# A four-layer conditional transformer: gelu once a job in place, its input added by VectorE, a plain float32 second product

## Time and profile before

| | us |
|---|---|
| median of 3 runs | 1162.45 |
| lowest, highest | 1158.63, 1163.27 |
| profiled execution: span | 1160.9 |
| TensorE busy (matmul records) | 1094.3 |
| TensorE weight loads | 703.3 |
| ScalarE busy | 800.4 |
| VectorE busy | 706.6 |
| GpSimd busy | 491.9 |

### The profile page before, as it was taken

The page is one execution under the profiler, slowest core; times in us unless marked ns, Lnnn a source line. Parts: engine busy times, 40 slices in busy tenths (PEclk is TensorE's granted clock), DMA queues, the critical chain, the costliest instruction groups (busy, mean ns, idle before and its releaser), DMA issues.

```text
span 1160.9 us, 19685 instructions
## 1 busy us (share of the span) xinstructions
PE 1094.3 (94%) x6717; PEld 703.3 (61%) x6717; DVE 706.6 (61%) x1484; ACT 800.4 (69%) x1336; POOL 491.9 (42%) x447
## 2 busy tenths in 40 slices
PE   8899999889898999999999999999999999999985
PEld 5576877655555565656657656566656566555442
DVE  6554447535256266234775865865865866898874
ACT  3563655477788778787687686687687686686763
POOL 3542742613543623644335553335344345254222
PEclk9999999899999999999999999999999999999997
DMA  7000001213222203321122231023031121232301
GB/s 234 20 26 28 2 10 31 62 38 94 60 64 73 75 1 82 84 58 35 28 75 73 69 83 42 15 65 82 23 88 29 39 55 51 56 84 55 83 12 36
DMA packets 36385, 64.45 MB, mean 56 GB/s; under 512 B 7208, under 2 KB 22312, under 8 KB 36288
## 3 DMA queue, kind: packets, MB, share of 16 engines
q1 hardware_dynamic: 36288, 63.20, 20.6%
HBM read 22.90 MB, written 2.12 MB: 22 GB/s over the span
## 4 chain that ended last, share of the span: by engine, by line
PE 73%; DVE 10%; ACT 8%; issue 6%; POOL 4%; POOLq 0%; ACTq 0%; DVEq 0%
PE rings L597 13%; PE AVB L709 13%; PE rings L598 11%; PE rings L599 11%; PE rings L696 10%; PE rings L671 5%; DVE m L1203 2%; PE rings L729 2%; ACT probs L891 2%; PE rings L734 2%; PE rings L640 1%; ACT L891 1%; DVE m L1183 1%; ACT gT_h L957 1%; PE rings L746 1%
## 5 line engine op out<-in xcount | busy, mean ns | idle before, releaser
L1203 DVE TENSOR_REDUCE m<-rings 128x1 fp32r<-128x512 f32 x512 | 319.0, 681 | 100.6 <-PE rings L671 73.3
L891 ACT ACTIVATE probs<-rings 128x512 f32<-128x512 f32 x562 | 292.9, 616 | 99.4 <-PE rings L671 71.1
L696 PE MATMUL rings<-SQ,SK 64*128 64x512 f32 x768 | 237.9, 446 | 14.7 <-ACT probs L888 6.3
L671 PE MATMUL rings<-SK,SQ 63*128 63x512 f32 x512 | 200.3, 457 | 5.4 <-ACT probs L891 4.2
L696 PEld LDWEIGHTS rings<-SQ,SK 64*128 64x128 f32 x768 | 109.0, 188 | 142.4 <-issue 55.1
L709 PE MATMUL AVB<-probs,V 128*32 128x512 f32 x1536 | 193.6, 611 | 0.0
L1306 POOL TENSOR_TENSOR gT_l<-gT_f,gT_h 128x512 fp32r<-128x512 f32 x96 | 121.4, 1286 | 75.7 <-ACT gT_h L957 73.8
L888 ACT ACTIVATE probs<-rings 128x1024 f32<-128x1024 f32 x103 | 101.0, 1037 | 34.2 <-PE rings L696 20.6
L597 PE MATMUL rings<-w_h,gT_h 128*128 128x256 f32 x384 | 110.2, 287 | 1.2 <-ACT gT_h L957 0.7
L671 PEld LDWEIGHTS rings<-SK,SQ 63*128 63x128 f32 x512 | 84.2, 184 | 39.7 <-ACT probs L891 33.1
L598 PE MATMUL rings<-w_l,gT_h 128*128 128x256 f32 x384 | 106.7, 278 | 0.0
(11 more groups left out here) (185 smaller groups left out, 2229.4 us busy)
## 6 DMA issues: line engine op xcount, KB each, us to landing
SQ<-qh SPq DMA_DIRECT2D x96, 128.0 KB, 2.6
SK<-kh SPq DMA_DIRECT2D x96, 128.0 KB, 2.8
SQ<-ql SPq DMA_DIRECT2D x48, 128.0 KB, 2.7
SK<-kl SPq DMA_DIRECT2D x48, 128.0 KB, 2.9
raw<-in_w SPq DMA_DIRECT2D x20, 256.0 KB, 2.8
wmod_s<-in_wmod SPq DMA_DIRECT2D x6, 512.0 KB, 4.1
gates<-gate_rows SPq DMA_DIRECT2D x12, 256.0 KB, 3.6
raw<-in_wqkv SPq DMA_DIRECT2D x9, 256.0 KB, 2.8
```

Of the source, the lines that this page charges most:

```text
L671: mm = pe.matmul(o[:, :], SQ[a % 4][r:r + KS, n // 2, c * P:(c + 1) * P], SK[a % 4][r:r + KS, n // 2, :], start=True, stop=True)
L696: mm = pe.matmul(o[:, :], SK[a % 4][r:r + KS + 1, n // 2, c * P:(c + 1) * P], SQ[a % 4][r:r + KS + 1, n // 2, :], start=True, stop=True)
L891: act.activation(probs[:, n % PROBS, :], bank(kind, a, i)[:, :], ACT.Exp, scale=SCALE[layer(unit_job(a))]).then_inc(done["scores"], 1)
L1203: nc.vector.tensor_reduce(m16[:, col:col + 1], bank(kind, a, i)[:, :], AX_X, ALU.max, negate=True).then_inc(done["max"], 1)
```

## The change

1. **Gelu.** `fc1` is now a step of VectorE too: it adds the bias and writes each bank to `gT` (eight chunks, full float32). One step `gelu` a job applies the gelu in place, four times to two chunks (128x1024). There is no `gT_h`, no `gT_l`, no GpSimd part.
2. **Second product.** `fc2` has four steps, one a token tile, each of 8 plain float32 matmuls of 256 columns in one bank; w2 is loaded straight to `w2_s`, without division. VectorE adds the bias once (128x256); GpSimd takes two tiles at a time, as before.
3. **hT.** In layers 0 to 2 ScalarE writes only the full copy, VectorE copies it to the rounded part, and GpSimd takes the difference after that.
4. **Layer 0.** A step `merge` forms Wv·Wp with a split product and puts it in the place of Wv; `mergerow` forms bv·Wp and adds it to the projection's bias. V is then already projected. `av0` and its evictions fall away; `proj` of layer 0 is 16 plain matmuls of 256 columns of transposed probabilities and V. The host hands Wv over transposed.
5. **Root.** VectorE computes the reciprocal root itself, from an integer first guess and three steps of three operations; `qkrs` falls away and ScalarE takes no part.
6. **Banks.** While layer 0 runs, the ring has eight banks, `AVB` among them.
7. **Order.** All tables of times and all patterns are replaced; two of them are shown.

```diff
+ROOT_SEED, ROOT_STEPS = 0x5f3759df, 3
...
-FFN = {"hT2": (23.5, 23.91), "fc1": (25.6, 25.81, 25.82, 25.83, 29.55, 29.56, 29.57, 29.58), "gelu": (25.84, 29.59),
-       "fc2a": (27.45, 29.55), "fc2": (30.55, 31.2)}
...
+FFN = {"hT2": (23.38, 23.43), "fc1": (25.08, 25.27, 25.67, 25.79, 27.39, 28.31, 28.58, 28.87), "gelu": (28.94,),
+       "fc2": (29.4, 31.32, 31.65, 34.38)}
...
-PAIR = ("p6 A p6 0 p6 1", "p4 A p6 0 p4 1", "p8 A p2 0 p8 1", "p6 A p6 0 p6 1", "p6 A p8 0 p4 1", "p6 A p8 0 p6 1", "p6 A p8 0 p4 1", "p6 A p8 0 p4 1")
...
+PAIR = ("a p10 b 0 p214 1", "0 p4 a p8 1 b", "a 0 p10 b p222 1", "0 p4 A p8 1", "0 1 p10 A", "0 a p14 b p66 1",
+        "p4 a p6 b p16 0 1 p14", "p6 A p6 0 1")
...
-        gT_h = sb("gT_h", [P, MT // 2, TOK], F32R)
-        qk = over("qk", [P, 4, TOK])
-        gT_l = sb("gT_l", [P, MT // 2, TOK], F32R)
-        gT_f = over("gT_f", [P, MT // 2, TOK])
+        gT = sb("gT", [P, MT, TOK])
+        qk = gT[:, 0:4, :]
...
+        ring = [rings[:, TOK * i:TOK * i + TOK] for i in range(RING + 1)]
+        AVB = ring[RING]
...
+        def by_vector(a):
+
+            return layer(a) < LAYERS - 1
...
-                elif kind == "av0":
-                    pe.wait_ge(done["pT0"], nth("pT0", a, TT - 1))
+                elif kind == "merge":
+
+                    pe.wait_ge(done["split_qkv"], nth("split_qkv", 0, 2))
+                    pe.wait_ge(done["split_wp"], 1)
+                    for c in range(CH):
+                        for k in range(CH):
+                            off = 2 * DIM + c * P
+                            mm = product(o[:, c * DIM:(c + 1) * DIM], [w[:, k, off:off + P] for w in (wqkv_h, wqkv_l)],
+                                         [w[:, k, :] for w in (wp_h, wp_l)], k == 0, k == CH - 1)
+                elif kind == "mergerow":
+
+                    pe.wait_ge(vb_ready, 1)
+                    pe.wait_ge(done["split_wp"], 1)
+                    for c in range(CH):
+                        for w in (wp_h, wp_l):
+                            mm = pe.matmul(o[:, 0:DIM], tok2[:, c, 0:P], w[:, c, :].bitcast(F32),
+                                           start=(c == 0 and w is wp_h), stop=(c == CH - 1 and w is wp_l))
+                elif kind == "proj" and not multi(a):
                     pe.wait_ge(done["v"], nth("v", a, 1))
-                    for t in range(TT):
-                        mm = pe.matmul(o[:, :], V[a % 2][:, t, i * P:(i + 1) * P], oU[:, t, :],
-                                       start=(t == 0), stop=(t == TT - 1))
+                    for t in range(2):
+                        pe.wait_ge(done["pT0"], nth("pT0", a, 2 * i + t))
+                        tok = (2 * i + t) * P
+                        for k in range(TT):
+                            mm = pe.matmul(o[:, t * DIM:(t + 1) * DIM], oU[:, k, tok:tok + P], V[a % 2][:, k, 0:DIM],
+                                           start=(k == 0), stop=(k == TT - 1))
                 elif kind == "oT1":
...
-                elif kind in ("fc2a", "fc2"):
-
-                    h = int(kind == "fc2")
-                    for t in range(2):
-                        tok = (2 * i + t) * P
-                        for m in range(MT // 2):
-                            if i == 0 and t == 0:
-                                pe.wait_ge(g_lo, (nth("gelu", a, h) - 1) * (MT // 2) + m + 1)
-                                pe.wait_ge(done["split_w2"], nth("split_w2", layer(a), 2 * h + m // 2))
-                            mm = product(o[:, t * DIM:(t + 1) * DIM], [x[:, m, tok:tok + P] for x in (gT_h, gT_l)],
-                                         [w[:, h * MT // 2 + m, :] for w in (w2_h, w2_l)], m == 0, m == MT // 2 - 1)
+                elif kind == "fc2":
+
+                    for m in range(MT):
+                        if i == 0:
+                            pe.wait_ge(gated, (nth("gelu", a) - 1) * (MT // 2) + m // 2 + 1)
+                            pe.wait_ge(in_w2[m // 2], 16 * (layer(a) + 1))
+                        mm = pe.matmul(o[:, 0:DIM], gT[:, m, i * P:(i + 1) * P], w2_s[:, m, :], start=(m == 0), stop=(m == MT - 1))
...
+                    for dst in (full[:, i, :],) if by_vector(a) else (full[:, i, :], hi[:, i, :]):
...
-                elif kind == "qkroot":
-
-                    act.wait_ge(ss_ready, nth(kind, a))
-                    act.activation(rs[:, :, :], ss[:, :, :], ACT.Sqrt).then_inc(done[kind], 1)
...
-                    if i == 0 and READ_BEFORE[(kind, a, i)]:
-                        act.wait_ge(pe_ring, use(*READ_BEFORE[(kind, a, i)]))
-                    if i == 1:
-                        act.wait_ge(pe_ring, use("fc2a", a, 1))
-                    elif a > 0:
-                        act.wait_ge(pe_ring, use("fc2", a - 1, 1))
-                    else:
-
-                        act.wait_ge(done["split_w1"], nth("split_w1", 0, 3))
-                    for m in range(i * MT // 2, (i + 1) * MT // 2):
-                        act.wait_ge(pe_ring, use("fc1", a, m))
-                        col = C_B1 + m
-                        for dst in (gT_f, gT_h):
-                            ins = act.activation(dst[:, m % (MT // 2), :], bank("fc1", a, m)[:, :], ACT.Gelu,
-                                                 bias=colv[:, layer(a), col:col + 1])
-                        ins.then_inc(done["fc1"], 1)
+                    for m in range(0, MT, 2):
+                        act.wait_ge(done["fc1"], nth("fc1", a, m + 1))
+                        act.activation(gT[:, m:m + 2, :], gT[:, m:m + 2, :], ACT.Gelu).then_inc(gated, 1)
...
+                elif kind in ("hT1", "hT2") and by_vector(a) and (kind, a, i) not in EARLY:
+                    dve.wait_ge(hi_in[kind], nth(kind, a, i))
+                    full, hi = [x[:, i, :] for x in ((hT_f, hT_h) if kind == "hT1" else (postT_f, postT_h))]
+                    nc.vector.tensor_copy(hi, full).then_inc(rounded[kind], 1)
...
-                    nc.vector.tensor_scalar(ss[:, :, :], ss[:, :, :], 1e-24, None, ALU.max).then_inc(ss_ready, 1)
-                elif kind == "qkrs":
-
-                    dve.wait_ge(done["qkroot"], nth("qkroot", a))
-                    link(nc.vector.reciprocal(rs[:, :, :], rs[:, :, :]))
+                    if nth(kind, a) > 1:
+                        dve.wait_ge(kbar_ready, nth("k", a - 1, CH - 1) - CH * BATCH)
+                    link(nc.vector.tensor_scalar(ss[:, :, :], ss[:, :, :], 1e-24, None, ALU.max))
+                    link(nc.vector.tensor_scalar(rs[:, :, :].bitcast(I32), ss[:, :, :].bitcast(I32), 1, None,
+                                                 ALU.arith_shift_right))
+                    link(nc.vector.tensor_scalar(rs[:, :, :].bitcast(I32), rs[:, :, :].bitcast(I32), -1, ROOT_SEED,
+                                                 ALU.mult, ALU.add))
+                    for _ in range(ROOT_STEPS):
+                        link(nc.vector.tensor_tensor(root[:, :, :], rs[:, :, :], rs[:, :, :], ALU.mult))
+                        link(nc.vector.scalar_tensor_tensor(out=root[:, :, :], in0=root[:, :, :], scalar=-0.5, in1=ss[:, :, :],
+                                                            op0=ALU.mult, op1=ALU.mult))
+                        link(nc.vector.scalar_tensor_tensor(out=rs[:, :, :], in0=root[:, :, :], scalar=1.5, in1=rs[:, :, :],
+                                                            op0=ALU.add, op1=ALU.mult))
...
+                elif kind == "fc1":
+
+                    dve.wait_ge(pe_ring, use(kind, a, i))
+                    if i == 0:
+                        if READ_BEFORE[(kind, a, i)]:
+                            dve.wait_ge(pe_ring, use(*READ_BEFORE[(kind, a, i)]))
+                        if a > 0:
+                            dve.wait_ge(pe_ring, use("fc2", a - 1, TT - 1))
+                        else:
+                            for step in PIECES[:4]:
+                                dve.wait_ge(done[step[0]], nth(*step))
+                    nc.vector.tensor_scalar(gT[:, i, :], bank(kind, a, i)[:, :], colv[:, layer(a), C_B1 + i:C_B1 + i + 1], None,
+                                            ALU.add).then_inc(done[kind], 1)
+                elif kind == "fc2":
+                    dve.wait_ge(pe_ring, use(kind, a, i))
+                    for step in TMP_BEFORE[(kind, a, i)]:
+                        dve.wait_ge(done[step[0]], nth(*step))
+                    dve.wait_ge(in_rowp, 16 * (layer(a) + 1))
+                    nc.vector.tensor_tensor(tmp[:, i, :], bank(kind, a, i)[:, 0:DIM], rowp[:, R_FB:R_FB + DIM], ALU.add
...
-                elif kind == "gelu":
-
-                    for m in range(MT // 2):
-                        pool.wait_ge(done["fc1"], nth("fc1", a, i * MT // 2 + m))
-                        nc.gpsimd.tensor_tensor(gT_l[:, m, :], gT_f[:, m, :], gT_h[:, m, :].bitcast(F32), ALU.subtract
-                                                ).then_inc(g_lo, 1)
...
```

(2 more changed lines are left out.)

299 lines of the change are left out of this document (164 added, 135 removed), and 13 rows, old and new, of tables (FIRST, SINGLE0, START).

## The result

The changed kernel takes **1112.07 us** (median of 4 runs, 1111.13 to 1113.09) against 1162.86 for the kernel before, run beside it (1158.63 to 1163.61): ratio 0.9564, 95% interval 0.9543 to 0.9584. That is 4.4% or 51 us faster. The forecast was 1151 and the range ended at 1122: the sign was right, the size was not.

What follows compares the result with a forecast made beforehand. TensorE was taken as the bound, with some 300 us of the chain elsewhere. 1160.9 + 27.2 (TensorE) - 5 - 35 + 3 - 2 = 1149.1, plus 1.5 to the runs' median: 1151 us, range 1122 to 1184.

Steps and rivals of the forecast that it cites:

- the stock, 300 us of the chain: Whole kernel before: some 300 us of the chain of waits are not TensorE's work; any gain must come from them.
- Second product, +34.9: Feed-forward second product on TensorE: plain float32 instead of split products, 13.8 instead of 10.8 us a job, +34.9 us in all.
- Layer 0, +3.1 - 10.8 - 5: Layer 0: merging weights adds 3.1 us, dropped split projection products save 10.8, a removed step between products saves 5.
- the +5 named as an end: Layer 0, first 60 us: worst end of the -5 term, +5 us if the merge before V delays the first job's products.
- ScalarE and GpSimd, -35: Lighter gelu, hT and subtraction work on ScalarE and GpSimd shortens the path by 35 us: about 26 and 9.
- VectorE, +3: Added evictions and copies, 73 us of VectorE work in all, are mostly hidden and cost 3 us (0 to +30).
- Rival (3): VectorE becomes the wait of layers 1 and 2, evictions and blocked copies before the maxima: +20 to +30, 1173 us; 10%.
- Gelu step, open rest of 1 us: Between fc1 and fc2: ScalarE's 6.7 us beside 4.1 + 3.4 us of TensorE leave 1 us open, within the +3.
- The copies and the shared port: 46 VectorE copies each wait 0.2 us on average for GpSimd's port, 9 us on VectorE, left off the path.
- Root, -2: Layer 1 variance root moved from ScalarE to VectorE: -2 us (-8 to +6) over four jobs.
- The signs I had named: Profile after: gelu loads 12, ACT near 660, DVE 780, POOL 360, TensorE's chain share 77% or more, plus window lengths.
- Rival (4): ScalarE was the hidden bound of layers 0 to 2: 65 us return instead of 35, 1121 us; 10%.

Runs made afterwards that it cites:

- experiment 6: Two runs on the kernel before: VectorE copy replaces each chunk's second gelu activation, 1157.84 us; identity replaces gelu, so its table loads go, 1151.78 us.

## Why the prediction was wrong

The step that failed is the last sentence before the rivals: of the new order "the rows can't price it, and it widens the range by some 10 us either way". For the new code the order is worth 101 us (1213.35 to 1112.07), 39 by the tables of the lead and 74 by those of the windows, 46 of these by one table. The rest of the sum failed too, the other way: the code was put at 12 us less and measured 49 more in the old order. The two misses, 61 and 101 us, partly cancel, so that the forecast's sign is right and its distance is 39 us is luck. I took a list of times for a detail because the rows of before show no time for it. They do show the stock, 300 us of the chain that weren't TensorE's, and I drew on it for the relief of ScalarE and GpSimd, not for the order.

By the steps:

- *Second product, +34.9*: right. 768 records, 0.216 apart; the time follows at 0.83, +29 in the old kernel. Taken at full value it was 6 us too much.
- *Layer 0, +3.1 - 10.8 - 5*: wrong in the old order, where the merged layer 0 costs 7.6 instead of giving 12.7; the merge waits 6.5 us for `wp_l`, as the +5 named as an end had it, and the transposes wait 6.7 more on `qk`. In the new order the first wait is gone and lead and first window are 38 us shorter than in the old.
- *ScalarE and GpSimd, -35*: wrong as a mechanism. In the old order 52 and 50 us less ScalarE gave 6.1 and 11.5. The waits on exponentials that I took as the nearest measure did fall: at the product of the earlier trace rows from 33.1 to 10.5 us in the whole kernel, over all lines from 76.4 to 39.1. With all the relief and the old order they stay at 33.9 and 66.5. GpSimd's part had no run to itself.
- *VectorE, +3*: it got 89 us of work instead of 73, and its price depends on the place. With the steps in the old clumps VectorE's share of the chain is 17% and TensorE waits 68.6 us on the maxima; spread out, 13% and 56.2. An extra microsecond costs 0.45 even there. Rival (3) named this mechanism, evictions ahead of the maxima; the new order takes back part of it.
- *Gelu step, open rest of 1 us*: too careful: the sum's own 6.7 us beside 7.5 leave no rest, the trace has no gap before the second product, and the removal of the loads gives 0.
- *The copies and the shared port*: right in its number by luck. The two rows below (count; then busy us, mean ns) make 29.6 us for 46 copies, 0.64 each; their median is 0.43, so some 0.2 a copy is blocking, as estimated. The estimate took the rule of the Trainium skill's "SBUF — State Buffer", section "Who interferes with whom", that whoever comes first holds the shared ports for the whole instruction, and spread it over GpSimd's busy share. The trace agrees with the rule and not with the spreading: nine of the copies last 1.38 to 1.42 us and most of the others 0.41 to 0.48. The nine are second copies of a pair, and what blocks them is GpSimd's subtraction for the first copy, begun just before (third and fourth lines). To leave it off the path was borne out as far as a run shows: the copies on VectorE, blocked as they are, are 8 us better than on ScalarE, which lacks the reserve.

```profile
L1047 DVE CAST postT_h<-postT_f 128x512 fp32r<-128x512 f32 x24 | 17.3, 729 | 6.4 <-ACT postT_f L872 6.3
...
L1047 DVE CAST hT_h<-hT_f 128x512 fp32r<-128x512 f32 x22 | 12.3, 563 | 25.3 <-ACT hT_f L872 25.3
```

```profile
636.49 1.29 POOL L1369 TENSOR_TENSOR postT_l<-postT_f,postT_h 128x512 fp32r<-128x512 f32 x1 [6.83 <-DVE postT_h L1047]
636.65 1.41 DVE L1047 CAST postT_h<-postT_f 128x512 fp32r<-128x512 f32 x1 [0.24 <-ACT postT_f L872]
```

- *Root, -2*: nothing measurable.

Put together from the runs: 1163 + 29 (plain product) + 8 (merged layer 0) = 1200; the new code in the old order has 1213, so what is left, evictions on VectorE, the one gelu step, the root and the relief, comes to +13 as a remainder that no run splits, where the prediction had -35 + 3 - 2 = -34; the order then takes 101. The signs I had named read 12 gelu loads, ACT 662.5, DVE 795.9, POOL 355.7, TensorE 80%, ScalarE and GpSimd 3% instead of 9%, layer 2 windows 81.2 to 83.3 (82 to 84 named), and layer 1 windows of 70.4, 76.7, 80.8 and 74.3 (79 to 81 named): layer 2 within 1 us of what was named, and most of the miss in the lead and the first window. Rival (4), 1121 with "fuller clock in the first stretches", came nearest in its number and place, yet its cause, ScalarE as the hidden bound, is not borne out: experiment 6 gives about 18 us for 100 where it wanted 65 for 132.

What stays open: the old order had to be translated for the new code (one gelu step for two halves), so a better translation would make the structure's 49 us less and the order's 101 by as much, and the old code's 85 hangs on its translation too; and which of the other tables carries the waits on the exponentials wasn't tried one by one.

## What to carry to other kernels

Where every engine walks one written list, the list is a part of the change like any other. Take the waits inside the bound engine's span as the stock it can draw on, and expect code and list to fit only each other: here the code cost time in the old order, and the windows' order cost time under the old code. Before you read a run of a changed list, check that the step has really changed places; a new time alone moves nothing. A relief of a neighbouring engine pays only as far as the waits in its *present* order allow; take it away in one run (here the gelu's table loads) before counting on it. And "busy 60%" did not mean reserve here: add a small load and see at what rate the time follows.

## What the runs showed that was not expected

- One table load costs 1.283 us in every trace; removing 24 of them from the kernel after gave 0 us, and adding 24, with 12 dummies of 0.2 us, cost 28 to 30. What a load costs to add says nothing of what it gives back when it goes.
- Plain float32 with 256 columns runs as two records of 0.216 us whether the weights are the old kernel's rounded parts or full float32: 377/379 ns (least, median) at both lines, and the weight loads, 190 ns (median), don't widen the spacing.
- TensorE's time at the lower clock level goes with code and order together: the mean granted clock was 0.983 before, 0.993 after, 0.96 with the new code in the old order and 0.946 with the old code in the windows' new order.
- A wait laid to a missing input can be a place in another engine's list: the 6.5 us for `wp_l` are GpSimd standing at another job's variance.
